# Two blocks of the folded weights in one transfer: four weight transfers of 512 KB in place of eight of 256 KB

## The reference, cut to what matters

```python
Q = einsum('btx,dx->btd', layernorm(x), Wq) + bq
K = einsum('bpx,dx->bpd', ctx, Wk) + bk
attn = softmax(einsum('btd,bpd->btp', Q, K) / sqrt(512))
x = x + einsum('btp,bpd->btd', attn, ctx)          # the values are the context itself
h = layernorm(x)
x = x + experts(h) + shared_expert(h)              # top-4 routing by sigmoid scores
```

## Time and profile before

| | us |
|---|---|
| median of three runs | 531.44 (530.27 to 532.05) |
| the profiled execution | 529.8 |
| its span on the core | 527.5 |
| around the span | 2.3 |
| TensorE busy | 476.1 (90%) |
| VectorE busy | 261.0 (49%) |
| ScalarE busy | 150.3 (28%) |
| GpSimd busy | 123.3 (23%) |

### The profile page before, as it was taken

The page is one execution under the profiler, slowest core; times in us unless marked ns, Lnnn a source line. Parts: engine busy times, 40 slices in busy tenths (PEclk is TensorE's granted clock), DMA queues, the critical chain, the costliest instruction groups (busy, mean ns, idle before and its releaser), DMA issues.

```text
span 527.5 us, 10464 instructions
## 1 busy us (share of the span) xinstructions
PE 476.1 (90%) x2445; PEld 284.5 (54%) x2446; DVE 261.0 (49%) x753; ACT 150.3 (28%) x269; POOL 123.3 (23%) x134
## 2 busy tenths in 40 slices
PE   3989999999999999999779987999989999899970
PEld 1445344363636354353327665677766766677750
DVE  3214146273644445372636877555556557645420
ACT  0001112020303021020222435445455545534320
POOL 1000000000000000000000245354645553655531
PEclk9999999999999999999889999999999999999985
DMA  8999999999999999999945566998758776555642
GB/s 212 395 420 425 389 425 417 407 423 402 424 400 424 406 421 417 408 425 424 406 161 167 114 234 142 311 236 221 196 120 240 180 226 177 104 89 114 103 58 37
DMA packets 28231, 149.04 MB, mean 283 GB/s; under 512 B 4072, under 2 KB 4200, under 8 KB 16424
## 3 DMA queue, kind: packets, MB, share of 16 engines
q1 hardware_dynamic: 15832, 123.08, 58.9%
q0 software_dynamic: 8720, 20.21, 20.3%
q10 hardware_dynamic: 3664, 5.57, 3.4%
HBM read 133.84 MB, written 15.01 MB: 282 GB/s over the span
## 4 chain that ended last, share of the span: by engine, by line
PE 73%; DMA 11%; issue 5%; DVE 3%; ACT 3%; ACTq 1%; POOLq 1%; DVEq 0%; POOL 0%; SPq 0%
PE b L724 19%; PE scores L576 16%; PE b L600 15%; DMA out<-y_sb,add_at 7%; PE b L564 6%; PE b L527 4%; PE scores L724 4%; PE scores L539 2%; PE b L590 2%; DMA h_rows<-h 1%; DMA w_qk<-in_wk 1%; PE b L747 1%; PE b L613 1%; DMA taken<-h_rows,take_at 1%; ACT w_hi L944 1%
## 5 line engine op out<-in xcount | busy, mean ns | idle before, releaser
L600 PE MATMUL b<-ctx_rows,probs_t 125*64 125x512 f32 (+1 forms) x384 | 87.4, 606 | 0.0
L576 PE MATMUL scores<-ctx_cols,g_t 128*64 128x500 f32 x384 | 85.0, 586 | 0.9 <-DVE g_t L1102 0.9
L445 POOL TENSOR_TENSOR rstd<-var_eps,neg_half 128x1 f32<-128x1 f32 x16 | 8.8, 550 | 268.2 <-DVE var_eps L1064 268.2
L486 POOL DMA_INDIRECT out<-y_sb,add_at x34 | 57.4, 1688 | 57.5 <-issue 22.9
L1331 DVE TENSOR_TENSOR w_lo<-w_raw,w_hi (+1 forms) x33 | 39.7, 1223 | 44.7 <-ACT w_hi L944 43.0
L724 PE MATMUL b<-w_hi,taken_hi 128*128 x136 | 54.6, 402 | 1.1 <-ACT taken_hi L955 1.1
L724 PE MATMUL b<-w_lo,taken_hi 128*128 x136 | 53.8, 396 | 0.0
L600 PEld LDWEIGHTS b<-ctx_rows,probs_t 125*64 125x64 f32 (+1 forms) x384 | 26.7, 140 | 49.2 <-issue 48.3
L576 PEld LDWEIGHTS scores<-ctx_cols,g_t 128*64 128x64 f32 x384 | 26.2, 136 | 48.0 <-issue 46.6
L469 POOL DMA_INDIRECT taken<-h_rows,take_at x34 | 34.2, 1005 | 39.4 <-issue 26.2
L944 ACT CAST w_hi<-w_raw (+1 forms) x33 | 33.8, 1049 | 24.9 <-PE scores L724 9.0
(11 more groups left out here) (229 smaller groups left out, 683.3 us busy)
## 6 DMA issues: line engine op xcount, KB each, us to landing
ctx_rows<-in_ctx SPq DMA_DIRECT2D x48, 1024.0 KB, 16.1
ctx_cols<-in_ctx_t SPq DMA_DIRECT2D x32, 1500.0 KB, 19.2
w_raw<-in_experts SPq DMA_DIRECT2D x11, 1536.0 KB, 7.1
h_rows<-h ACTq DMA_DIRECT2D x16, 115.5 KB
taken<-h_rows SPq DMA_DIRECT2D x7, 264.0 KB, 2.9
out<-xs ACTq DMA_DIRECT2D x2, 784.0 KB
shared_raw<-in_shared SPq DMA_DIRECT2D x1, 1536.0 KB, 27.0
xs<-in_x ACTq DMA_DIRECT2D x12, 112.0 KB
```

Of the source, the lines that this page charges most:

```text
L486: nc.gpsimd.indirect_dma_start(out[:, :], bass.IndirectOffsetOnAxis(ap=add_at[i][:, 0:1], axis=0), y_sb[:, i * DIM:(i + 1) * DIM], None, c ...
L576: last = nc.tensor.matmul(scores[HALF * b:HALF * (b + 1), n, 0:CHUNK], g_t[:, k, HALF * b:HALF * (b + 1)], ctx_cols[:, at:at + CHUNK], sta ...
L600: last = nc.tensor.matmul(b3[HALF * b:HALF * (b + 1), :], probs_t[0:rows_in(p), at:at + HALF], ctx_rows[0:rows_in(p), g, b, c * DIM:(c + 1 ...
```

## The change

The eight transfers become four: each moves two adjacent blocks of one weight, 4 KB per partition in place of 2 KB. There are two semaphores `w_loaded` in place of four. TensorE waits before block 0 until blocks 0 and 1 of both weights have landed, and before block 2 for blocks 2 and 3; the waits before blocks 1 and 3 are met already. The products and their order stay.

```diff
-        w_loaded, b_loaded, sh_loaded = [sem(f"w_loaded{k}") for k in range(KD)], sem("b_loaded"), sem("sh_loaded")
+        w_loaded, b_loaded, sh_loaded = [sem(f"w_loaded{k}") for k in range(KD // 2)], sem("b_loaded"), sem("sh_loaded")
...
-            for k in range(KD):
-                sp.dma_start(wq_sb[:, k, :], wq[:, k, :]).then_inc(w_loaded[k], 16)
-                sp.dma_start(wk_sb[:, k, :], wk[:, k, :]).then_inc(w_loaded[k], 16)
+            for k in range(0, KD, 2):
+                sp.dma_start(wq_sb[:, k:k + 2, :], wq[:, k:k + 2, :]).then_inc(w_loaded[k // 2], 16)
+                sp.dma_start(wk_sb[:, k:k + 2, :], wk[:, k:k + 2, :]).then_inc(w_loaded[k // 2], 16)
             load_x(sp, 0)
             load_x(sp, 1)
...
                 for k in range(KD):
-                    pe.wait_ge(w_loaded[k], 32)
+                    pe.wait_ge(w_loaded[k // 2], 32)
```

## The result

| | before | after |
|---|---|---|
| median of 22 runs, us | 532.27 (530.27 to 536.55) | 533.94 (531.29 to 536.67) |
| profiled execution, us | 529.8 | 532.57 |
| its span, us | 527.5 | 530.3 |
| TensorE's first matmul, us | 8.29 | 11.24 |
| TensorE ready for the first `taken`, us | 267.88 | 271.67 |

The ratio after to before is 1.0035 (95% interval 1.0019 to 1.0051). Times 532 us that is 1.9 us slower; the two medians lie 1.7 us apart. The forecast was 0.3 us faster, and the time lies 0.4 us above the range. Part of this last distance is the base: the forecast was added to a median of 531.44, and the larger set of runs puts the kernel before at 532.27. So of the 2.8 us between 531.1 and 533.94, 0.8 are the base, and 2.0 to 2.2 are what the reasoning had wrong.

A forecast was written before the change was run, and what follows sets the result against it. It took TensorE's back-to-back work as the bound, with the DMA stream close behind, both meeting near 268 us. Restart +0.5 us and clock -0.8 gave -0.3 on a median of 531.44: 531.1 us, range 528.6 to 533.5.

The forecast's parts named there:

- The first matmul: At the kernel's start: TensorE's first matmul comes 2.6 us later, at 10.9 us (9.8 to 12.0).
- the gain: In the first weight transfers: larger packets give back at most 2.2 us of a 3.7 us delay; 1.1 taken.
- rival 1: First weight transfers: the price is per packet, so TensorE starts only 1.5 us later; total 529.0 us; chance 0.22.
- rival 3: First weight transfers: joining does nothing to the packets, TensorE starts 3.7 us later; total 532.2 us; chance 0.10.
- The cover before block 2: In the fold: the wait before block 2 costs nothing, with 4.4 us between landing and use.
- The dry spell: Queue q1 after about 58 us: it runs dry for 1.0 us, leaving the stream 0.1 us behind.
- Both shifts: TensorE 2.6 us late and the context stream 1.1 us early, together 3.7 us, meeting at the second round's first row reload.
- the slack: Queue q1 at the second round's first row reload: 2.7 us before it runs dry, 2.1 at least.
- The seam: Store of `h` and reload of `taken`, about 270 us: 2.1 us of TensorE's delay swallowed, restart 0.5 us late.
- rival 2: Store of `h`: keeps its 8.6 us, the whole delay passes on, +2.6 us, total 534.0 us; chance 0.18.
- The clock: TensorE behind the wait for `taken`: a pause of 1.1 us should keep the clock up, worth -0.8 us.
- The tail and the other engines: Everything behind 277 us keeps its length and moves along; VectorE, ScalarE and GpSimd only shift with TensorE.

The follow-up runs named there:

- swap_after: The changed kernel with the last pair's third attention group moved ahead of the transpose of the first `taken` tile; ratio to the kernel before 0.9998.
- wait_all: The kernel before with its eight transfers, but TensorE waits for all four blocks of both weights ahead of block 0; ratio to the kernel before 1.0122.
- early_after: The changed kernel with the shared expert's weights (1.5 MB) loaded at about 51 us, ahead of the first row reload; ratio to the kernel before 0.9970.
- pad_late_after: The changed kernel with the padding of x held back until blocks 0 and 1 have landed; ratio to the kernel before 0.9993.
- join_late: The kernel before with only blocks 2 and 3 joined, blocks 0 and 1 in single transfers; ratio to the kernel before 1.0036, repeated 1.0002.
- quiet_start: The kernel before with GpSimd's zero writes and ScalarE's transfers behind the constants waiting until block 0 has landed; ratio to the kernel before 0.9988.
- quiet_after: The changed kernel with GpSimd's zero writes and ScalarE's transfers behind the constants waiting for blocks 0 and 1; ratio to the kernel before 1.0072.
- control: The kernel before run again unchanged, to show scatter; ratio to the kernel before 1.0000.

## Why the prediction was wrong, point by point

**The first matmul: right in its range, the gain too large.** 11.24 in 9.8 to 12.0. The joining gave back 0.7 us of the 3.7, and I had taken 1.1. The argument was right in part, and partly by luck. Over the first 9 us a joined packet did take less than two single ones (234 against 2 x 166 ns), and q1 moved 0.35 MB more. But the two microseconds from which I took the price do not show it (505 against 277 ns, 142 against 75), and the price is none of the packet as such: with the padding held back a 2 KB packet took 91 ns, and the joining moved no more bytes. So this lies between rival 1 and rival 3. The prediction also set 8.25 us against the 4.4 of the Trainium skill, "DMA: Bandwidth & Descriptors", section "Anatomy of one DMA". That section has its fit from transfers that GpSimd issues. The weights are issued by SyncE, beside other transfers, so this is no test of the page.

**The cover before block 2: right.** The last weight landed at 14.9, needed at 20.5. SyncE's queue is free at 2.67, as worked out.

**The dry spell: right in its place, too small.** The queue was dry for 2.4 us, not for 1.0. Both shifts were larger, TensorE's 3.37 us and the stream's lead 1.1, 4.5 in place of 3.7. And the slack was 4.5 - 2.4 = 2.1 us, not 2.7; it was the lower bound that I had given. The term at fault is the 1.9 us for what lies before a block's first packet and behind its last: the row block that met an empty queue took 5.0 us, and 1 MB at 0.42 MB a microsecond is 2.5 of them, which leaves 2.5. So the stream is 1.3 us late behind the gap, and not 0.1 early. No wait for the last columns came, as TensorE was later still.

**The seam: this is the step that failed.** I let the landing of the store lie between a quiet 4.4 us and a loaded 8.56 and took the middle, 6.5; it took 7.43. In relation to the store q1 ended 3.8 - 0.9 = 2.9 us earlier (its last large transfer, `shared_raw`, landed at 270.2 against 269.3), somewhat more than the 2.6 that I had; of this 1.1 came back, and I had taken 2.1. Two things were overlooked. That last transfer still lands 6.5 us behind the store's issue, so the quiet price was out of reach, and a middle between the two ends had no meaning. The other kernels bear this out: the store took 7.43 to 7.56 us where `shared_raw` landed 6.5 to 6.7 us behind its issue (after, swap_after, wait_all), 8.1 to 9.3 where it landed 7.6 to 9.6 behind (the fifteen others in which it ends the stream), and 6.04 and 6.49 where it was loaded early. And the first packets of this store come 3 us and more after its issue, which q1's earlier end did not change; in early_after, with 1.5 MB less in q1, they came within 2.8 us. Queue q10 by microseconds, in the kernel before from 263 to 264 us, with nothing in the one ahead:
```profile
q10 hardware_dynamic: 17, 0.04, 9.2%
```
and in the changed kernel from 267 to 268, with nothing in the one ahead:
```profile
q10 hardware_dynamic: 40, 0.08, 20.6%
```
Issued at 259.91 and 263.69, the first packets lie at least 3.1 and 3.3 us behind, and only the part behind them shrank, from at most 5.5 us to at most 4.1. The reload took 0.16 us more. TensorE was to start 0.5 us late and started 2.82 late. It is rival 2 in direction and place, though with 7.43 us the store lies a hair under the 7.5 from which I had let it decide, and the pause went down by 1 us, as that rival did not have it.

**The clock: not given back, because the pause was too long.** I had put -0.8 us on a pause of 1.1 us. The pause was 2.35 us, and the clock fell as before (5.28 us for the 16 matmuls). The idea behind the term holds in the runs: of the 15 profiled executions with the old order at the seam, the two with the shortest pauses, 1.15 us (early_after) and 2.25 (pad_late_after), kept the clock (3.58), and the 13 with pauses of 2.35 to 3.75 us all lost it (4.7 to 6.1 us for the 16). So this term failed with the store's price and not by itself. (A slip of the prediction: 0.5 + 1.2 is 1.7 and not 1.6.)

**The tail and the other engines: right.** Plan to end is 221.7 and 221.6 us.

**The sum again, with what was measured:** +2.95 at the start, 0.43 of cold stretch and 0.4 within attention, less 1.0 at the seam gives 2.8, the difference of the two spans. By the ratio it is 1.9. The 0.8 of cold stretch and attention are of the size by which executions of one kernel differ, and without them 2.95 - 1.0 = 1.95. Against the forecast of -0.3, these 1.95 are a miss of 2.25 us: 0.35 is the start (2.95 for 2.6), 1.1 the seam (0.93 of the store, 0.16 of the reload), and 0.8 the clock that hung on it.

**What stays open.** Why a store waits over 3 us for its first packet; why 16 packets of 16 KB slow all the weights' packets so much; and whether join_late's 1.0036 was chance, for which its repetition speaks, or whether joining has a small cost beside the late start.

## What to carry to other kernels

Joining transfers gains only as much as the packets get cheaper, and it moves the first use back to the landing of the whole. Here that was 0.7 us against 3.7. At the start of a kernel it is a cost, unless something else lands later still. Where compute and a stream of transfers are both nearly full, look on which side the slack is: a late start cost some two thirds of its delay or more, and an early start gained nothing that could be measured, since the stream then set the end. Do not take the middle between a loaded and a quiet price: work out how long the load lies beside the transfer, and what of its price comes before its first packet.

## What the runs showed of the hardware

Two transfers of 128 KB on 8 partitions, in another queue, delayed the first 512 KB of weights: the first matmul started at 7.9 to 8.7 us with them and at 5.2 to 5.9 without, while GpSimd's zeros did nothing to them (8.69 with the zeros held back). Beside these transfers packets of 4 KB moved 1.17 to 1.20 MB in 9 us, where packets of 2 KB moved 0.81 to 0.84; without them both moved 1.65 MB. A load of 2 KB took 9.8 us in the kernel before, 14.5 in quiet_start, where it was issued at 6.60 us behind the padding in its own queue and just ahead of the context in q1, and 18.7 in quiet_after, issued at 8.13 with the context already under way. The clock at the seam fell behind every pause of 2.35 us or more and behind neither of the two shorter ones. How long it then stayed low differs between executions of one kernel: the sixteen matmuls took 4.74 us in the kernel before and 5.95 in control, and over all kernels the first six matmuls took from 4.25 to 5.67 us.
